# LayerNorm's negated mean and variance plus epsilon as free-axis sums over a table with an epsilon column

## The reference

```python
def _layernorm(x, axis=-1, eps=1e-05):
    m = jnp.mean(x, axis=axis, keepdims=True)
    v = jnp.var(x, axis=axis, keepdims=True)
    return (x - m) / jnp.sqrt(v + eps)
...
    x = x + _L0_xattn_ref(_layernorm(x, axis=-1), ctx_768, ...)
    x = x + _L0_ffn_ref(_layernorm(x, axis=-1), ...)
    x = x + _L1_xattn_ref(_layernorm(x, axis=-1), ctx_768, ...)
    x = x + _L1_ffn_ref(_layernorm(x, axis=-1), ...)
```

## Time and profile before

| what | value |
|---|---|
| median of 3 runs | 231.06 us |
| the profiled execution's own time | 231.44 us |
| its span, first to last instruction | 229.6 us |
| TensorE matmul busy | 223.2 us, 97% |
| VectorE / ScalarE / GpSimd busy | 164.1 / 152.8 / 126.4 us |
| granted TensorE clock, mean over the span | 0.998 |

### The profile page before, as it was taken

One profiled execution on the slowest core, in us unless ns is written; L12 is line 12 of the kernel. 1 busy time (PEld: TensorE's weight loads), 2 busy tenths in 40 slices (PEclk: granted clock), 3 DMA queues, 4 the chain that ended last, 5 costly groups with the idle time before them and its releaser, 6 DMA issues.

```text
span 229.6 us, 4315 instructions
## 1 busy us (share of the span) xinstructions
PE 223.2 (97%) x1389; PEld 166.7 (73%) x1389; DVE 164.1 (71%) x482; ACT 152.8 (67%) x376; POOL 126.4 (55%) x127
## 2 busy tenths in 40 slices
PE   7999999999999999999999999999999999999994
PEld 3576765965889898889535563588878888888883
DVE  3689984788667963699948983564867785776874
ACT  2579999986679445672689778876464554645561
POOL 2866742899046927857492107208499500996540
PEclk9999999999999999999999999999999999999999
DMA  6790000000029925900600000027000003700002
GB/s 207 202 302 7 0 3 0 0 3 1 3 80 238 370 105 148 218 3 4 217 3 3 3 1 6 0 67 305 0 0 0 3 0 97 274 0 4 0 0 91
DMA packets 10172, 17.04 MB, mean 74 GB/s; under 512 B 3715, under 2 KB 5540, under 8 KB 9766
## 3 DMA queue, kind: packets, MB, share of 16 engines
q1 hardware_dynamic: 9926, 16.45, 23.0%
q10 hardware_dynamic: 224, 0.32, 0.4%
HBM read 16.08 MB, written 0.62 MB: 73 GB/s over the span
## 4 chain that ended last, share of the span: by engine, by line
PE 86%; ACT 6%; DVE 4%; POOL 2%; issue 1%; DVEq 0%; POOLq 0%
PE psum L1181 12%; PE psum L1185 11%; PE psum L1182 11%; PE psum L1354 7%; ACT prob L749 5%; PE psum L1416 5%; PE psum L1362 4%; PE psum L1364 3%; PE psum L1363 3%; PE psum L1472 3%; PE psum L1300 3%; PE psum L1312 3%; PE psum L1437 2%; PE psum L1276 2%; PE psum L1189 2%; PE psum L1460 2%
## 5 line engine op out<-in xcount | busy, mean ns | idle before, releaser
L703 POOL TENSOR_TENSOR act_s<-act_s,spread 128x512 f32<-128x512 f32 x35 | 44.3, 1289 | 20.2 <-DMA spread<-cw 14.1
L1181 PE MATMUL psum<-xT_hi,w_hi 128*128 128x512 f32 x108 | 43.9, 406 | 0.0
L1185 PE MATMUL psum<-xT_lo,w_hi 128*128 128x512 f32 x108 | 42.3, 391 | 0.0
L1182 PE MATMUL psum<-xT_hi,w_lo 128*128 128x512 f32 x108 | 42.1, 390 | 0.0
L798 ACT CAST q<-psum 128x512 fp32r<-128x512 f32 x35 | 20.4, 587 | 21.4 <-PE psum L1364 15.1
L1009 DVE TENSOR_TENSOR q<-psum,q 128x512 fp32r<-128x512 f32 x35 | 23.8, 687 | 13.5 <-ACT q L798 13.0
L788 ACT ACTIVATE act_s<-psum 128x512 f32<-128x512 f32 x39 | 23.1, 597 | 12.3 <-PE psum L1185 7.9
L1152 DVE TENSOR_REDUCE neg_max<-psum 128x2 f32<-128x308 f32 x64 | 26.2, 472 | 4.6 <-PE psum L1416 4.4
L703 POOL TENSOR_TENSOR hid<-hid,spread 128x512 f32<-128x512 f32 x13 | 16.5, 1286 | 18.7 <-DMA spread<-cw 14.4
L652 POOL TENSOR_TENSOR rstd<-vareps,minus_half 128x4 f32<-128x4 f32 x8 | 8.1, 1018 | 33.4 <-DVE vareps L910 33.4
L646 POOL TENSOR_TENSOR w_lo<-w_src,w_hi 128x768 fp32r<-128x768 f32 x12 | 21.8, 1835 | 8.6 <-ACT w_hi L718 8.6
(11 more groups left out here) (173 smaller groups left out, 467.0 us busy)
## 6 DMA issues: line engine op xcount, KB each, us to landing
spread<-cw SPq DMA_DIRECT2D x16, 256.0 KB, 4.6
spread<-cw SPq DMA_DIRECT2D x6, 512.0 KB, 5.6
w_src<-in_w SPq DMA_DIRECT2D x2, 1152.0 KB, 5.1
w_src<-in_w SPq DMA_DIRECT2D x1, 2304.0 KB, 10.9
spread<-cw SPq DMA_DIRECT2D x8, 128.0 KB, 2.9
w<-in_w SPq DMA_DIRECT2D x1, 576.0 KB, 6.6
out<-X SPq DMA_DIRECT2D x4, 128.0 KB, 1.8
wv<-in_wv SPq DMA_DIRECT2D x2, 192.0 KB, 4.8
```

The source lines that it names most:

```text
L703: pool.tensor_tensor(g, g, spread[:, slot, :], ALU.mult).then_inc(weighed, 1)
L1181: pe.matmul(dst, w_hi, xT_hi[:, b, :], start=True, stop=False)
L1182: pe.matmul(dst, w_lo, xT_hi[:, b, :], start=False, stop=False)
L1185: return pe.matmul(dst, w_hi, xT_lo[:, b, :], start=False, stop=True)
```

## The change

Three things are in the diff.

1. The table `mv` has a third column, filled once with epsilon by a `memset` at the program's start. `bn_aggr` writes columns 0 and 1. `neg_mean` is now a `tensor_reduce` with `negate` over column 0 alone, one element for each token tile, and `vareps` a `tensor_reduce` over columns 1 and 2, two elements for each token tile. Both are sums. The instructions on either side are the same.
2. A function `need` keeps, for each engine and semaphore, the highest count that was waited for, and issues a wait only for a higher one. `wait_filled` and `wait_moved` go through it, and some waits that were issued under conditions (`if first`, `if j == 0`) are now asked for at each step and pass through `need`.
3. The wait behind the residual add of sublayer 1 (`res`) moved to the head of the next `lnA`, which is the next VectorE step in both places.

```diff
-        mv = sb("mv", [P, B, T, 2])
+        mv = sb("mv", [P, B, T, 3])
...
+        reached = {}
+
+        def need(eng, semaphore, n):
+
+            at = (id(eng), id(semaphore))
+            if n > reached.get(at, 0):
+                eng.wait_ge(semaphore, n)
+                reached[at] = n
+
         def wait_filled(eng, key):
             k, n, _ = uses[key]
-            eng.wait_ge(bank_ready[k], n)
+            need(eng, bank_ready[k], n)
...
         def wait_moved(eng, key):
-            eng.wait_ge(*reads_of(key))
+            need(eng, *reads_of(key))
...
             dve.memset(act_s[:, 0, :], 0.0).then_inc(idle_ready, 1)
+            note(dve.memset(mv[:, :, :, 2], EPS))
...
+                    if s == 2:
+                        wait_moved(dve, ("y", 1, b))
                     settle()
...
-                        note(dve.bn_aggr(mv[:, b, t, :], stats[:, b, t, :]))
+                        note(dve.bn_aggr(mv[:, b, t, 0:2], stats[:, b, t, :]))
                     settle()
-                    note(dve.tensor_scalar(neg_mean[:, b, :], mv[:, b, :, 0], -1.0, None, ALU.mult))
-                    dve.tensor_scalar(vareps[:, b, :], mv[:, b, :, 1], EPS, None, ALU.add).then_inc(var_ready, 1)
+                    note(dve.tensor_reduce(neg_mean[:, b, :], mv[:, b, :, 0:1], AX, ALU.add, negate=True))
+                    dve.tensor_reduce(vareps[:, b, :], mv[:, b, :, 1:3], AX, ALU.add).then_inc(var_ready, 1)
...
                     moved(dve.tensor_tensor(xb, bank(key).rearrange("p (t d) -> p t d", t=T), xb, ALU.add), key)
-                    wait_moved(dve, key)
...
-            def product3(dst, w_hi, w_lo, s, b, first):
-                if first:
-                    pe.wait_ge(xT_rounded, position[("xT", s, b)])
+            def product3(dst, w_hi, w_lo, s, b):
+                need(pe, xT_rounded, position[("xT", s, b)])
                 pe.matmul(dst, w_hi, xT_hi[:, b, :], start=True, stop=False)
                 pe.matmul(dst, w_lo, xT_hi[:, b, :], start=False, stop=False)
-                if first:
-                    wait_moved(pe, ("xT", s, b))
+                wait_moved(pe, ("xT", s, b))
...
```

More of the change, by code:

```diff
@@ L1196, in _ @@
                     p = step[1]
-                    if p == 0:
-                        pe.wait_ge(loaded["ctx"], 16 * N_CTX)
+                    need(pe, loaded["ctx"], 16 * N_CTX)
                     filled(pe.matmul(bank(step)[:, 0:B * CP], wk0[:, p * P:(p + 1) * P],
@@ L1237, in _ @@
                     s, b = step[1:]
-                    if (s, b) == (0, 0):
-                        pe.wait_ge(loaded["ident"], 16)
+                    need(pe, loaded["ident"], 16)
                     for t in LN_ORDER:
@@ L1245, in _ @@
                     b, p = step[1:]
-                    if (b, p) == (0, 0):
-                        pe.wait_ge(lo_of["wq0"], 1)
+                    need(pe, lo_of["wq0"], 1)
                     c = slice(p * P, (p + 1) * P)
-                    filled(product3(bank(step), wq_hi0[:, c], wq_lo0[:, c], 0, b, p == 0), step)
+                    filled(product3(bank(step), wq_hi0[:, c], wq_lo0[:, c], 0, b), step)
                 elif kind == "scores":
@@ L1385, in _ @@
                     g = step[1]
+                    need(pe, loaded["ctx"], 16 * N_CTX)
+                    need(pe, loaded["kv1"], 16 * N_KV1)
                     filled(pe.matmul(bank(step)[:, 0:B * CP], wk1[:, g, :], ctxT[:, :, :].rearrange("k b c -> k (b c)"),
@@ L1388, in _ @@
                 elif kind == "qd":
-                    if step[1] == 0:
-                        pe.wait_ge(lo_of["wq1"], 1)
-                    filled(product3(bank(step), wq_hi1[:, :], wq_lo1[:, :], 2, step[1], True), step)
+                    need(pe, lo_of["wq1"], 1)
+                    filled(product3(bank(step), wq_hi1[:, :], wq_lo1[:, :], 2, step[1]), step)
                 elif kind == "q1":
```

19 lines of the change are left out of this document (8 added, 11 removed).

## The result

The changed kernel took 233.01 us (median of 4 runs, 232.47 to 233.25), the kernel before 231.06 us beside it (4 runs, 230.94 to 231.5). The ratio is 1.0072, with a 95% interval of 1.0055 to 1.009. By the ratio it is slower by 1.7 us (1.3 to 2.1 us by the interval; the two medians lie 1.95 us apart), and outside the predicted range. The profiled execution took 232.95 us with a span of 231.2 us, 1.6 us more than the 229.6 us of before.

What follows compares the result with a forecast made beforehand. TensorE's matmuls were taken to bound the kernel (busy 97% of the span), hiding most other work. Reduces 0, memset and moved wait 0, waits -0.1 us gave 230.96, rounded to 231.0 us, range 230.3 to 231.6 us.

Steps and rivals of the forecast that it cites:

- the sum: Whole kernel: 0 for reduces, 0 for memset and moved wait, -0.1 us for waits, giving 231.0 us.
- a shift in how the engines' phases meet: Leftover case, engines' phases meeting differently in either direction: chance 0.04, 0.02 each way.
- The sixteen exchanged instructions: LayerNorm's pair on VectorE, in the chain at two of eight passages: 0 us, bounds -0.06 and +0.06 us.
- The memset and the moved wait: VectorE at program start and behind sublayer 1's residual add: both hidden or unchanged, 0 us each.
- The waits: Waits no longer issued, 47 on TensorE and 25 on ScalarE: mostly hidden, -0.1 us, gain between 0 and 0.7 us.
- at most one 51 ns: TensorE behind the true wait at L1424: three semaphores named instead of four, so one wait's issue time at most is gained.
- The argument that TensorE's sequencer runs ahead of the array: TensorE before L1354 at 90.95 us: sequencer leads by more than 51 ns, so dropped waits are mostly hidden.
- The first: Rival on TensorE's short idle stretches: ten to fourteen dropped waits fully exposed, 0.5 to 0.7 us gained, 230.5 us; chance 0.23.
- The second: Rival at 46 and 112 us: dearer, non-overlapping reduces cost 0.35 us more at each place, 231.7 us; chance 0.13.
- The third: Rival for the whole kernel: dropped waits all hidden, reduces cost the same, 231.06 us; counted within the forecast's 0.60.
- the third of the conditions for being wrong: TensorE's full stretches: the prediction called itself wrong if the matmuls' pitch there changes.
- One of the signs: GpSimd's softmax normalization L676, before 51 us: should start within 0.05 us of 48.70.

Runs made afterwards that it cites:

- e4: Kernel before with only the dropped and moved waits (`need`); `mv` keeps two columns, every tile its old place: 231.67 us, ratio 1.0013.
- e1: Changed kernel plus 32 unused bytes behind `mv`, so tiles behind start 64 bytes further on than in the kernel before: 232.98 us, ratio 1.0072.
- e11: Changed kernel with `real_rows` and `minus_half` made one tile, so nearly all tiles start where they did in the kernel before: 231.61 us, ratio 1.0011.
- e12: Changed kernel plus 224 unused bytes behind `mv`, so tiles behind start 256 bytes further on than in the kernel before: 231.52 us, ratio 1.0013.
- e2: Kernel before with only 32 unused bytes added behind `mv`, putting later tiles where the changed kernel has them: 233.12 us, ratio 1.0071.
- e3: Kernel before with only the third column, memset and sixteen reduces, plus a pad putting tiles behind `mv` 64 bytes on: 233.07 us, ratio 1.0074.
- e5: Kernel before with 128 unused bytes added behind `mv`: 232.57 us, ratio 1.0055.
- e9: Kernel before with `xT_hi` and `xT_lo` moved 32 bytes on and all tiles behind them 128 bytes on: 233.49 us, ratio 1.0092.
- the two small kernels: Not variants of the layer kernel: only TensorE runs, 23 segments of 30 512-column matmuls at varied offsets, marked by 64-column matmuls; 6.91 to 7.13 us per segment.

## Why the prediction was wrong

**The step that failed** is the sum. It adds up the exchanged instructions, the memset and the waits (0, 0 and -0.1 us) and so puts the pace of TensorE's own matmuls at 0 without a reason, since "nothing moved here" in the order on the engines. The third column of `mv` was priced as its `memset` alone. It has a second effect, the places of the tiles behind it, which no term held: 512-column matmuls at 233 to 234 ns instead of 227. That is worth 1.6 to 1.7 us, all of the result within the intervals: with the tiles in their old places the change measures 1.0011 [0.9993, 1.0028], and the places alone 1.0071 [1.0046, 1.0095]. Of the 0.04 left for "a shift in how the engines' phases meet", none fits: this is no matter of phases.

**The sixteen exchanged instructions: 0, right.** 157 and 151 ns measured, 148 and 152 ns estimated. The pair took 0.23 us, 0.02 us less than before at each of the two places, inside the bounds of -0.06 to +0.06 us for both. The reading of the earlier trace rows, mostly fixed time and overlap, held. The Trainium skill's rule on `tensor_reduce` ("VectorE: DVE Perf Modes", "Rules for kernel authors") would have made the pair dearer by 8 ns, by the estimate from it in the prediction. At these sizes the trace does not agree: the reduces are shorter than the `tensor_scalar` that they replace.

**The memset and the moved wait: 0, right.** The memset took 65 ns at 1.3 us, and the next work of VectorE starts at 3.63 us, against 3.65 us in the earlier trace rows.

**The waits: -0.1 us, the wrong sign.** e4 measures 1.0013 [0.9996, 1.0031], so a gain of more than 0.04% (0.1 us) is outside its interval. The traces say more, since five of them have the changed waits (the changed kernel, e1, e4, e11, e12) and eight have those of before. At the place of the earlier trace rows it takes 240 to 253 ns from L1185 to L1424 in the five and 307 to 340 ns in the eight, and at 136 us, from L1499 to L1424, 166 to 170 ns against 257 to 265 ns. In e4:

```profile
116.46 0.40 PE L1191 MATMUL psum<-xT_lo,wq_hi 128*128 128x512 f32 x1
116.70 0.10 PEld L1429 LDWEIGHTS psum<-ident,neg_max 128*32 128x32 f32 x1 [0.28 <-DVE neg_max L1161]
```

VectorE's maximum, the true wait there, ends 0.16 to 0.20 us after L1185 starts in all thirteen, so it is not the reason. Behind a true wait, then, a dropped one gave 0.09 us, more than the "at most one 51 ns" of the prediction. But at 67 us the same waits cost. From L1185 over four transposes to the next L1181 the kernel before takes 0.58 us, and e4, from its L1191 to its L1188, 0.79 us:

```profile
67.03 0.39 PE L1185 MATMUL psum<-xT_lo,w_hi 128*128 128x512 f32 x1
67.26 0.60 PE L1242 MATMUL psum<-ident,xn 128*128 128x128 f32 x4
67.61 0.47 PE L1181 MATMUL psum<-xT_hi,w_hi 128*128 128x512 f32 x1
```

```profile
66.47 0.39 PE L1191 MATMUL psum<-xT_lo,w_hi 128*128 128x512 f32 x1
66.77 0.73 PE L1245 MATMUL psum<-ident,xn 128*128 128x128 f32 x4
67.26 0.48 PE L1188 MATMUL psum<-xT_hi,w_hi 128*128 128x512 f32 x1
```

It is 0.75 to 0.79 us in all five and 0.58 to 0.59 us in all eight. Why is open. Over the steps from 12 us on in which all five differ from all eight, by 15 ns or more at the median, the gains and losses add up to 0.18 us lost. Whole executions show no more than a hint of it: e4, e11 and e12 came out at 1.0011 to 1.0013, and only the interval of e12, from 1.0001, excludes 1. The argument that TensorE's sequencer runs ahead of the array holds for most places, not for the one at 67 us.

**The rivals.** The first (the waits pay 0.5 to 0.7 us) falls with e4, though two places did pay. The second, on the other side, gave 231.7 us for a pair of 0.60 us at each place; the pair took 0.23 us. The sign came out as the second rival's, by a mechanism that is not its own. The third, exactly nothing, is within the interval when the places are kept (e11).

**What would show it.** "If the matmuls' pitch in the full stretches changes" was the third of the conditions for being wrong, and it is the one that came true. The count of the last stretch in the earlier trace rows, 379, and the pitch of 0.23 us in the earlier trace rows were in hand. What was missing was the question on what that pitch rests. One of the signs did not come out: GpSimd's L676 (L685 now) starts at 48.46 us, 0.24 us before 48.70 where 0.05 was allowed. That is the lead from the start of the program, and not the pair.

**The mechanism.** Shown: the pitch of a 512-column matmul behind another, each with weights of its own, is 227 ns where the weights and the moving operand lie a multiple of 256 bytes apart (16 bytes more or less), and 229 to 234 ns elsewhere, with no other engine at work. It looks as if weight loads and the streaming operand meet somewhere in SBUF. The Trainium skill says otherwise ("TensorE: Matmul & The Clock Gate", "Step-by-step: what each phase is for"): "Loading the next tile's weights doesn't steal SBUF read bandwidth from the running matmul." If the two do meet there, the 6 ns a matmul (2.7%) of the segments above speak against that sentence. But that is my reading and not shown: no run streams the same operand without loading weights, so what the distance acts on stays open.

**What stays open.** The rule is on a stream of matmuls and not on each pair by itself: L1362 to L1364 keep their distance in the changed kernel, in e1, e2, e3, e5 and e9, and are slower in each. In the two small kernels the step behind a mark takes some 310 to 320 ns, and then a good layout needs up to 12 matmuls until it is back at 227 ns (224 to 239 ns meanwhile), so three matmuls between slow ones may never settle. That fits, and it was not tested. Why 64 bytes cost 233 ns and -64 or 192 bytes 229 ns is not settled. Between 58 and 95 us the change costs 0.26 us. Most of that is that fewer 512-column pairs run there, 83 against 280 from 145 to 225 us, but they also lose less, 3.1 ns each against 4.9. The kernel before is itself at a mean of 228.4 ns (L1182 to L1185) and 230.6 ns (L1185 to L1181) there. A stream that is not settled may be that too.

No variant beats the kernel before. The change with its tiles in place or 256 bytes on is as fast, within 0.3%.

## What to carry to other kernels

An edit that changes the size of a small tile can move every tile allocated behind it, so a price for it starts with a list of addresses before and after, not only with the instructions. In a kernel bound by TensorE, take the start-to-start time of its commonest matmul, in ns, and the count in a full stretch as numbers of their own: busy time and idle time hide a change of 3%. Where 512-column matmuls of type `F32R` each load new weights, keep the weights and the moving operand a multiple of 256 bytes apart in a partition; unused bytes can restore it (e12), and until a move of tiles is ruled out, a difference of 0.7% says nothing on the edit itself.

## What the hardware showed that I had not expected

- The 256-byte rule: 227 ns against 229 to 234 ns a matmul, with 6.94 and 7.10 us for 30 of them, in a kernel with all engines busy (227 against 233 to 234 ns) as in one with TensorE alone. It cost this kernel 1.7 us of 231.
- The pitch is a pattern of the layout and not noise. With TensorE alone it goes 231, 235, 232, 235 ns and on at 32 bytes, 229, 238, 229, 237 ns at 128 bytes, and 226, 229, 232 ns at -64 bytes.
- It hardly depends on the others. In the changed kernel from 145 to 225 us, the mean of the 512-column steps that lie wholly within ScalarE's work is 231.7 ns and of those wholly outside it 231.7 ns; 232.0 and 231.9 ns for VectorE, 232.1 and 232.0 ns for GpSimd.
- The matmuls of 128 columns in L1354 don't show it: their tiles moved by 32 bytes against each other too, and they keep 112 ns. They are of type `F32` and not `F32R`, so whether it is the size or the type is open.
- Waits that are satisfied can cost or save by where they stand: with 47 fewer on TensorE and 25 on ScalarE, two places on TensorE gained 0.09 us each and one lost 0.2 us.
